# Attention scores on a half-filled systolic array: 32-row bands, with keys and queries kept a second time in turned bands

## The chip, the core and the metric

The kernel runs on one core of a Trainium2 chip. Its engines are TensorE (PE; its weight loads are listed apart as PEld), VectorE (DVE), ScalarE (ACT), GpSimd (POOL) and SyncE (SP, which only issues transfers). The metric is the device time of one launch in microseconds, lower is better.

## What is computed

One block of a network: cross-attention from 2048 queries to 1601 context rows with 8 heads of 4 numbers each, added to x behind a gate, and then a layer of 8 experts that each take their 512 best rows.

```python
q = _split_heads(queries @ Wq + bq)     # 8 heads, 4 numbers each
k = _split_heads(keys @ Wk + bk)
v = _split_heads(values @ Wv + bv)
scores = jnp.einsum('bhqd,bhkd->bhqk', q, k) * scale
attn = jax.nn.softmax(scores, axis=-1)
o = jnp.einsum('bhqk,bhkd->bhqd', attn, v)
...
x = x + jnp.tanh(g_xattn[0]) * attention(_layernorm(x), ctx_1024, ctx_1024, ...)
x = x + jnp.tanh(g_ffn[0]) * experts(_layernorm(x), ...)
```

## The kernel before

The heads are taken in two groups g of four. A head's query and key are each split into three bf16 parts, so that bf16 products give float32 scores; with the row of its maximum a head takes 32 of the 128 partitions, so a group fills the 128. The tile `qrows` holds the queries in that form and `kpad` the keys.

Work is cut into 16 units: four chunks c of 512 queries, in each two groups, in each two halves h of 256 queries. The four units of a chunk are numbered r = 0 to 3. A unit runs over 13 key tiles kt of 128 keys (the last has 65), and in each of them PE does this, in the order written in the main loop at the end of the block of PE:

- the maxima that are due (`max_tile`), in front of the scores and behind them. A unit has 16 of them (`TILES`), dealt out over the 13 key tiles by `tiles_by`, about one unit ahead of their use. Each is two matmuls of 401 keys that fill two PSUM banks; DVE reduces both at once into `mquart` and frees them. Two such pairs of banks are in use (`next_dve`).
- the scores (`scores`, twice: p = 0 and p = 1). Each call makes two heads' scores, 256 queries each, into one bank, from which ACT makes `probs` by one exp of 512 columns. ACT's work has three banks in rotation (`next_act`): the call waits until ACT has emptied the bank it used three takings ago.
- the weighted sum of the values (`pv`) for the key tile two back, four heads side by side.

A contraction over 64 rows uses half of PE's rows: `band(p)` is rows 0 to 63 or 64 to 127. Two heads lie in a band, so `kpad` holds the keys twice, each time with one of the two heads cleared; DVE clears for group 0 (in `keys_split`), ACT for group 1 (`pad_k1`).

When a unit's maxima are complete, DVE turns them into rows (`max_parts`), PE adds them to the queries (`place_max`, at kt = 10 of the unit before) and ACT stores the sum as `qfull` (`q_full`).

Beside this, at fixed places (r, kt), runs the work of the neighbour chunks: transposes and projection of the next queries (`XN_AT`, `Q_AT`), output projection (`WO_AT`), second normalisation, transposes of x2 and the router (`X2_AT`, `ROUTER_AT`). All engines are in-order queues with waits on semaphores; nothing is reordered by a scheduler. Transfers are issued by SP in the order written.

Of the kernel before, what the change touches and what calls it, by code (L numbers as in the profile page):

```python
# [17 lines left out]
P = 128  # L18
# [90 lines left out]
def build(nc, x, ctxt, g_x, g_f, Wq, bq, Wk, bk, Wv, bv, Wo, bo, rw, rb, w1, b1, w2, b2, cf, cdigits, out, x2d):  # L109
# [9 lines left out]
    with es:  # L119
# [33 lines left out]
        kpad = ar("kpad", [P, NG, 2, KEYS], BF16)  # L153
# [3 lines left out]
        qfull = ar("qfull", [P, NG, CW], BF16)  # L157
# [6 lines left out]
        krows = ar("krows", [P, 2, CW], BF16)  # L164
# [33 lines left out]
        with nc.sbuf_tensor("ctx_sb", [P, NKT, D], F32) as ctx_sb, nc.sbuf_tensor("ctxT", [P, KD, KEYS], F32) as ctxT:  # L198
# [70 lines left out]
        s_xf, s_c1, s_t1, s_c2, s_rows, s_kpad0, s_kpad1 = [sem(n) for n in (  # L269
            "qk_biased", "qk_high", "qk_rest", "qk_middle", "qk_rows", "k_padded_group0", "k_padded_group1")]  # L270
# [69 lines left out]
        def band(p):  # L340

            return slice(64 * p, 64 * p + 64)
# [53 lines left out]
        def _(sp):  # L396
# [22 lines left out]
            sp.dma_start(b2b[:, :, :], b2.rearrange("e h -> (e h)").partition_broadcast(P)).then_inc(s_b2, 16)  # L419
# [8 lines left out]

            for half in range(2):
                load_w1(0, half)  # L430
                load_w2(0, half)
            with sp.Fori(0, LAST) as c:
                sp.wait_ge(s_x1, c + 1)
                sp.dma_start(out_v[:, bass.ts(c, CT), :], xs[:, bass.ts(c, CT), :]).then_inc(s_out1, 16)
                sp.wait_ge(s_x2, c + 1)
                sp.dma_start(x2_v[:, bass.ts(c, CT), :], x2[:, :, :]).then_inc(s_x2st, 16)
# [23 lines left out]
        def _(pool):  # L460
# [46 lines left out]
            for b, (lo, w) in enumerate(KB):  # L507
                split_rest(pool, nc.gpsimd, 5 + b, (5 + b) % 2, w)
                pool.wait_ge(s_kpad0, 4)
                at_least(pool, s_kpad1, b - 1)  # L510
                split_rows(pool, nc.gpsimd, 5 + b, w, krows[:, b % 2, 0:w])
# [127 lines left out]
        def _(act):  # L639
# [66 lines left out]
            def pad_k1(j):  # L706

                lo, w = KB[j]
                act.wait_ge(s_rows, 5 + j + 1)
                for b in range(2):  # L710
                    last = nc.scalar.activation(kpad[:, 1, b, lo:lo + w], krows[:, j % 2, 0:w], ACT.Copy,
                                                scale=cst[:, C_HEAD + b:C_HEAD + b + 1])
                last.then_inc(s_kpad1, 1)

# [15 lines left out]
            pad_k1(3)  # L730
# [150 lines left out]
        def _(dve):  # L881
# [12 lines left out]
            for w, r in ((wk_sb, wkr), (wq_sb, wqr)):  # L894
                for k in range(KD):
                    for g in range(NG):
                        last = nc.vector.tensor_copy(
                            r[:, k, g, :].rearrange("p (h j d) -> p h j d", h=HG, d=HD)[:, :, 0:6, :],
                            w[:, k, 16 * g:16 * g + 16].rearrange("p (h d) -> p h d", d=HD).unsqueeze(2).to_broadcast([P, HG, 6, HD]))

            for g in range(NG):
                for k in range(KD):
                    nc.vector.tensor_copy(wkr[:, k, g, :].rearrange("p (h r) -> p h r", h=HG)[:, :, ROW_V:],
                                          wv_sb[:, k, 16 * g:16 * g + 16].rearrange("p (h d) -> p h d", d=HD))
                nc.vector.tensor_copy(bqkr[:, NG + g, :].rearrange("p (h r) -> p h r", h=HG)[:, :, ROW_V:],
                                      bias_sb[:, 64 + 16 * g:64 + 16 * g + 16].rearrange("p (h d) -> p h d", d=HD))
            for j in range(2):
                for g in range(NG):
                    last = nc.vector.tensor_copy(
                        bqkr[:, NG * j + g, :].rearrange("p (h j d) -> p h j d", h=HG, d=HD)[:, :, 0:6, :],  # L910
                        bias_sb[:, 32 * j + 16 * g:32 * j + 16 * g + 16].rearrange("p (h d) -> p h d", d=HD).unsqueeze(2).to_broadcast([1, HG, 6, HD]))
# [67 lines left out]
            def keys_split(j):  # L979

                lo, w = KB[j]
                split(j, j % 2, w, 2, krows[:, j % 2, 0:w])
                dve.wait_ge(s_rows, j + 1)
                for b in range(2):
                    last = nc.vector.tensor_scalar(kpad[:, 0, b, lo:lo + w], krows[:, j % 2, 0:w],
                                                   cst[:, C_HEAD + b:C_HEAD + b + 1], None, ALU.mult)
                last.then_inc(s_kpad0, 1)
# [22 lines left out]
            def max_tile(n):  # L1010

                u, j = divmod(n, TILES)
                t, a, kq = j // (2 * QUARTERS), j // QUARTERS % 2, j % QUARTERS
                dve.wait_ge(s_mm, n + 1)
                b = next_bank()
                nc.vector.tensor_reduce(mquart[:, u % 2, t, a, :, kq], ps[:, b:b + 2, 0:MAXW], AX.X, ALU.max).then_inc(s_mr, 1)  # L1016
                if j == TILES - 1:
                    max_parts(u)

            def max_parts(u):  # L1020

                dve.wait_ge(s_mr, TILES * (u + 1))
                at_least(dve, s_mpl, u)

                def spread(t, row):
                    return t[:, :, :, row].rearrange("p t (b a) -> p t a b", a=2)

                nc.vector.tensor_reduce(spread(mparts, KROW_M), mquart[:, u % 2, :, :, :, :], AX.X, ALU.max, negate=True)
                nc.vector.tensor_reduce(nmax[:, :, :].rearrange("p t (b a) -> p t a b", a=2), mquart[:, u % 2, :, :, :, :], AX.X, ALU.max,
                                        negate=True).then_inc(s_nm, 1)  # L1030
                dve.wait_ge(s_nm, u + 1)
                nc.vector.tensor_tensor(mparts[:, :, :, KROW_M + 1], nmax[:, :, :], mparts[:, :, :, KROW_M], ALU.subtract).then_inc(s_mp, 1)
# [306 lines left out]
        def _(pe):  # L1339
# [99 lines left out]
            def max_tile(n):  # L1439

                u, j = divmod(n, TILES)
                c, g, h, r = unit(u)
                t, a, kq = j // (2 * QUARTERS), j // QUARTERS % 2, j % QUARTERS
                if j == 0 and h == 0:
                    pe.wait_ge(s_rows, rows_of(c, g))
                if n < 4:
                    pe.wait_ge(s_kpad0, n + 1)
                    pe.wait_ge(s_xf, 4)
                if (c, g, h, j) == (0, 1, 0, 0):
                    pe.wait_ge(s_kpad1, 4)  # L1450
                bank = next_dve((s_mr, n + 1))
                lo, q = MAXSTEP * kq, CW * c + UW * h + P * t
                for b in range(2):
                    last = mm(ps[:, bank + b, 0:MAXW], qrows[band(b), g, q:q + P], kpad[band(b), g, a, lo:lo + MAXW], start=True, stop=True)  # L1454
                last.then_inc(s_mm, 1)

            def place_max(u):
# [5 lines left out]
                mm(ps[:, bank, 0:UW], ident_bf[:, :], qrows[:, g, q:q + UW], start=True, stop=False, skip_group_check=True)  # L1463
                for t in range(UQ):
                    last = mm(ps[:, bank, P * t:P * t + P], mparts[:, t, :, :].rearrange("p h r -> p (h r)"), ident_bf[:, :],
                              start=False, stop=True, skip_group_check=True)
                last.then_inc(s_mpl, 1)

            def scores(u, kt, p):
# [7 lines left out]
                last.then_inc(s_sc, 1)  # L1477

            def pv(u, kt):
# [7 lines left out]
                for hh in range(HG):  # L1487
                    last = mm(ps[32 * hh:32 * hh + 32, PV, 0:UW], vp[0:w, kt, g, hh, :], probs[0:w, step % PROBS, hh, :],  # L1488
                              start=(kt == 0), stop=(kt == NKT - 1))
# [92 lines left out]
            for u in range(UNITS):  # L1582
# [197 lines left out]
```

## Time and profile before

| | |
|---|---|
| median of 3 runs | 595.6 us (595.19 to 595.64) |
| the profiled execution | 594.75 us, of which its span is 592.9 us |
| PE busy | 551.4 us (93%) |
| DVE busy | 444.1 us (75%) |
| ACT busy | 397.4 us (67%) |
| POOL busy | 196.8 us (33%) |

The span has three parts: up to about 48 us loads, projections of keys and the first maxima; from 48 to 344 us the 16 attention units; then the choice of rows and the experts. The busy shares are means over parts with different limits, so the stretches have to be looked at one by one.

### The profile page before, as it was taken

Reading aid. Unit: us, or ns where it says so; the run is one execution under the profiler, and the core shown is the slowest. Engines: PE = TensorE matmul, PEld = TensorE weight load, DVE = VectorE, ACT = ScalarE, POOL = GpSimd, SP = SyncE. Lnnn points to the kernel's source line nnn. Section 1 sums busy time; section 2 is a strip of 40 time slices with the busy share of each in tenths; the row PEclk is TensorE's granted clock in tenths of the full one; section 3 lists DMA queues with packets and bytes.
Section 4 is the critical chain, followed back from the end, with each engine's and each line's share of the span. In section 5 each row is a group of like instructions: output and inputs, shape, how many; then the busy total and the mean of one; then the engine's idle time right before and its main releaser. Section 6 shows DMA issues by size and latency. Waiting matters only on the chain.

```text
span 592.9 us, 12821 instructions
## 1 busy us (share of the span) xinstructions
PE 551.4 (93%) x5043; PEld 318.6 (54%) x5043; DVE 444.1 (75%) x811; ACT 397.4 (67%) x774; POOL 196.8 (33%) x193
## 2 busy tenths in 40 slices
PE   6798899998999989999999998899999999999994
PEld 4433333333333333333333344469889898898974
DVE  3889879996798967989897258746767868677541
ACT  2587789987888878898888830044665646655651
POOL 3058030024420063400158010240735626346234
PEclk9999999999999999999999999999999999999998
DMA  8600000000000000000000004122735556356133
GB/s 280 241 2 1 1 1 3 2 1 38 2 36 2 2 37 1 37 2 1 37 38 2 36 19 140 34 60 72 163 112 117 144 136 148 108 107 163 16 36 35
DMA packets 23807, 35.80 MB, mean 60 GB/s; under 512 B 3459, under 2 KB 16196, under 8 KB 23620
## 3 DMA queue, kind: packets, MB, share of 16 engines
q1 hardware_dynamic: 17604, 26.59, 13.8%
q0 software_dynamic: 6144, 8.39, 8.3%
q8 instruction: 40, 0.66, 0.5%
q14 instruction: 19, 0.16, 0.1%
HBM read 26.59 MB, written 8.39 MB: 59 GB/s over the span
## 4 chain that ended last, share of the span: by engine, by line
PE 67%; DVE 18%; ACT 5%; issue 4%; POOL 3%; DMA 1%; POOLq 0%; ACTq 0%; DVEq 0%; SPq 0%
PE ps L1719 15%; PE ps L1726 15%; PE ps L1488 12%; DVE mquart L1016 11%; PE ps L1475 6%; PE ps L1454 6%; PE ps L1384 2%; ACT probs L741 2%; PE ps L1345 2%; POOL xn L528 2%; PE ps L1360 1%; PE ps L1697 1%; PE ps L1672 1%; ACT osb L641 1%; PE ps L1513 1%
## 5 line engine op out<-in xcount | busy, mean ns | idle before, releaser
L1016 DVE TENSOR_REDUCE mquart<-ps 128x2 f32<-128x802 f32 x256 | 241.9, 988 | 33.4 <-PE ps L1454 30.2
L741 ACT ACTIVATE probs<-ps 128x512 f32<-128x512 f32 (+1 forms) x416 | 222.9, 599 | 24.0 <-PE ps L1475 20.8
L1488 PE MATMUL ps<-probs,vp 128*32 128x256 f32 (+1 forms) x1664 | 132.7, 391 | 4.5 <-ACT osb L641 4.5
L1454 PE MATMUL ps<-kpad,qrows 64*128 64x401 bf16 x512 | 90.6, 337 | 3.7 <-DVE mquart L1016 3.1
L1475 PE MATMUL ps<-qfull,kpad 64*128 64x256 bf16 (+1 forms) x832 | 89.8, 272 | 2.8 <-ACT x L762 0.9
L1313 DVE TENSOR_TENSOR h1l<-hf,h1h 128x512 fp32r<-128x512 f32 x64 | 44.4, 693 | 56.0 <-ACT hf L868 56.0
L867 ACT ACTIVATE h1h<-ps,b1T 128x512 fp32r<-128x512 f32 x64 | 44.0, 687 | 53.8 <-PE ps L1719 53.6
L1726 PE MATMUL ps<-w2h,h1h 128*128 128x256 f32 x256 | 73.8, 288 | 2.2 <-DVE h1l L1313 1.5
L1726 PE MATMUL ps<-w2l,h1h 128*128 128x256 f32 x256 | 72.4, 283 | 0.0
L1726 PE MATMUL ps<-w2h,h1l 128*128 128x256 f32 x256 | 72.3, 283 | 0.0
L1475 PEld LDWEIGHTS ps<-qfull,kpad 64*128 64x128 bf16 (+1 forms) x832 | 38.9, 96 | 48.2 <-ACT probs L741 25.1
L611 POOL DMA_INDIRECT out<-eo,idx_put x32 | 56.3, 1759 | 25.1 <-ACT eo L877 15.9
L1454 PEld LDWEIGHTS ps<-kpad,qrows 64*128 64x128 bf16 x512 | 26.3, 93 | 66.0 <-DVE mquart L1016 31.8
L1488 PEld LDWEIGHTS ps<-probs,vp 128*32 128x32 f32 (+1 forms) x1664 | 33.3, 108 | 51.3 <-ACT probs L741 34.0
L1726 PEld LDWEIGHTS ps<-w2h,h1h 128*128 128x128 f32 x256 | 48.8, 191 | 6.6 <-issue 4.7
L1719 PE MATMUL ps<-tokh,w1h 128*128 128x512 f32 x128 | 51.0, 398 | 0.0
L1719 PE MATMUL ps<-tokh,w1l 128*128 128x512 f32 x128 | 50.4, 394 | 0.0
L1719 PE MATMUL ps<-tokl,w1h 128*128 128x512 f32 x128 | 49.9, 390 | 0.0
L1726 PEld LDWEIGHTS ps<-w2l,h1h 128*128 128x128 f32 x256 | 48.9, 191 | 1.3
L1726 PEld LDWEIGHTS ps<-w2h,h1l 128*128 128x128 f32 x256 | 48.9, 191 | 0.0
L589 POOL DMA_INDIRECT toks<-x_rows,idx_get x32 | 32.0, 999 | 36.0 <-DVE idx_get L1291 24.9
L868 ACT ACTIVATE hf<-ps,b1T 128x512 f32<-128x512 f32 x64 | 43.7, 683 | 0.0
(198 smaller groups left out, 682.3 us busy)
## 6 DMA issues: line engine op xcount, KB each, us to landing
w1raw<-in_L_ffn_w SPq DMA_DIRECT2D x16, 512.0 KB, 4.6
w2raw<-in_L_ffn_w SPq DMA_DIRECT2D x16, 512.0 KB, 4.7
xs<-in_x SPq DMA_DIRECT2D x4, 512.0 KB, 7.7
ctx_sb<-in_ctx SPq DMA_DIRECT2D x3, 512.0 KB, 5.8
out<-xs SPq DMA_DIRECT2D x3, 512.0 KB, 2.6
x_rows<-x SPq DMA_DIRECT2D x3, 512.0 KB, 2.6
b2b<-in_L_ffn_b SPq DMA_DIRECT2D x1, 1024.0 KB, 11.1
out<-xs SPq DMA_DIRECT2D x2, 256.0 KB, 2.0
```

What stands on the lines that cost most here:

```text
L589: nc.gpsimd.indirect_dma_start(out=toks[:, t, :], out_offset=None, in_=x2d, in_offset=bass.IndirectOffsetOnAxis(ap=idx_get[:, t:t + 1], ax ...
L611: nc.gpsimd.indirect_dma_start(out=out_rows, out_offset=bass.IndirectOffsetOnAxis(ap=idx_put[:, t:t + 1], axis=0), in_=eo[:, t, :], in_off ...
L741: nc.scalar.activation(out_p, ps[0:w, next_bank(), :], ACT.Exp, scale=float(SCALE)).then_inc(s_ex, 1)
L867: nc.scalar.activation(h1h[:, f, :], ps[:, bank, :], ACT.Relu, bias=bias).then_inc(s_hh, 1)
L868: nc.scalar.activation(hf[:, f % 2, :], ps[:, bank, :], ACT.Relu, bias=bias).then_inc(s_hf, 1)
L1016: nc.vector.tensor_reduce(mquart[:, u % 2, t, a, :, kq], ps[:, b:b + 2, 0:MAXW], AX.X, ALU.max).then_inc(s_mr, 1)
L1313: nc.vector.tensor_tensor(h1l[:, f, :], hf[:, f % 2, :], h1h[:, f, :].bitcast(F32), ALU.subtract).then_inc(s_hl, 1)
L1454: last = mm(ps[:, bank + b, 0:MAXW], qrows[band(b), g, q:q + P], kpad[band(b), g, a, lo:lo + MAXW], start=True, stop=True)
L1475: last = mm(ps[0:w, bank, UW * b:UW * b + UW], kpad[band(p), g, b, P * kt:P * kt + w], qfull[band(p), g, UW * h:UW * h + UW], start=True, ...
L1488: last = mm(ps[32 * hh:32 * hh + 32, PV, 0:UW], vp[0:w, kt, g, hh, :], probs[0:w, step % PROBS, hh, :], start=(kt == 0), stop=(kt == NKT - 1))
L1719: last = mm(ps[:, UP_BANKS[f % 3], :], w[:, k, P * f:P * f + P], r[:, k, :], start=(m == 0), stop=(m == len(terms) - 1))
L1726: last = mm(ps[:, bank, a:a + D], h[:, f, P * t:P * t + P], w[:, f, :], start=(f == 0 and m == 0 and a == 0), stop=(f == NF - 1 and m == 2 ...
```

## The change

Now a band has 32 rows, one head. The scores use the bands at rows 0 and 32 (`score_band`), the maxima the bands at rows 64 and 96 (`max_band`). As each head must appear in both halves, the keys are kept as made (`kbands`) and with the halves exchanged (`kturned`), the queries likewise (`qrows`, and `qturned` in its upper half); SP's transfers from SBUF to SBUF make the turned copies. The cleared copies `kpad` and the operations that make them are gone. `qfull` holds two pairs of heads side by side in 64 partitions, so `place_max` and `q_full` handle 512 columns of 64 rows instead of 256 of 128. A unit's maxima are taken for the unturned heads first.

```diff
+        def score_band(p):
+            return slice(32 * p, 32 * p + 32)
+        def max_band(b):
+            return slice(64 + 32 * b, 64 + 32 * b + 32)
...
+            def turn_keys(j, g):
+                lo, w = KB[j]
+                sp.wait_ge(s_rows, BLOCKS.index(("k", j, g)) + 1)
+                sp.dma_start(kturned[64:P, g, lo:lo + w], kbands[0:64, g, lo:lo + w]).then_inc(s_kup[g], 16)
+                sp.dma_start(kturned[0:64, g, lo:lo + w], kbands[64:P, g, lo:lo + w]).then_inc(s_kdown[g], 16)
+            def turn_queries(c, g):
+                sp.wait_ge(s_rows, rows_of(c, g))
+                if c > 1:
+                    sp.wait_ge(s_mm, TILES * (PER_CHUNK * (c - 2) + PARTS * (g + 1)))
+                sp.dma_start(qturned[64:P, g, c % 2, :], qrows[0:64, g, CW * c:CW * c + CW]).then_inc(s_qt[NG * (c % 2) + g], 16)
...
-            def pad_k1(j):
-                lo, w = KB[j]
-                act.wait_ge(s_rows, 5 + j + 1)
-                for b in range(2):
-                    last = nc.scalar.activation(kpad[:, 1, b, lo:lo + w], krows[:, j % 2, 0:w], ACT.Copy,
-                                                scale=cst[:, C_HEAD + b:C_HEAD + b + 1])
...
-                take(qfull[:, g, UW * h:UW * h + UW], ps[:, next_bank(), 0:UW], s_qf)
+                take(qfull[0:64, g, :, UW * h:UW * h + UW], ps[0:64, next_bank(), :].rearrange("p (v q) -> p v q", v=2), s_qf)
...
-                split(j, j % 2, w, 2, krows[:, j % 2, 0:w])
-                dve.wait_ge(s_rows, j + 1)
-                for b in range(2):
-                    last = nc.vector.tensor_scalar(kpad[:, 0, b, lo:lo + w], krows[:, j % 2, 0:w],
-                                                   cst[:, C_HEAD + b:C_HEAD + b + 1], None, ALU.mult)
+                split(j, j % 2, w, 2, kbands[:, 0, lo:lo + w])
...
-                    last = mm(ps[:, bank + b, 0:MAXW], qrows[band(b), g, q:q + P], kpad[band(b), g, a, lo:lo + MAXW], start=True, stop=True)
+                    rows = max_band(b)
+                    queries = qrows[rows, g, CW * c + q:CW * c + q + P] if a else qturned[rows, g, c % 2, q:q + P]
+                    keys = (kbands if a else kturned)[rows, g, lo:lo + MAXW]
+                    last = mm(ps[:, bank + b, 0:MAXW], queries, keys, start=True, stop=True)
...
-                bank = next_act((s_ex, 2 * (NKT * u + kt) + p + 1))
-                for b in range(2):
-                    last = mm(ps[0:w, bank, UW * b:UW * b + UW], kpad[band(p), g, b, P * kt:P * kt + w],
-                              qfull[band(p), g, UW * h:UW * h + UW], start=True, stop=True)
+                rows = score_band(p)
+                return mm(ps[0:w, bank, UW * v:UW * v + UW], (kturned if v else kbands)[rows, g, P * kt:P * kt + w],
+                          qfull[rows, g, v, UW * h:UW * h + UW], start=True, stop=True)
...
-                    scores(u, kt, 0)
-                    scores(u, kt, 1)
+                    first, second = score_bank(u, kt, 0), score_bank(u, kt, 1)
+                    scores(u, kt, 0, 0, first)
+                    scores(u, kt, 1, 0, second)
+                    scores(u, kt, 0, 1, first).then_inc(s_sc, 1)
+                    scores(u, kt, 1, 1, second).then_inc(s_sc, 1)
```

PE before, one key tile of unit 0 that has a maximum in front of the scores (`mquart`'s source, L1454) and one behind; the four L1475 are the scores, L1488 is `pv`, and `probs_ready` is the semaphore by which ACT gives banks and probabilities free.

```order
L1454 MATMUL ps<-kpad,qrows 128x401 [waits max_reduced]
L1454 MATMUL ps<-kpad,qrows 128x401
L1475 MATMUL ps<-qfull,kpad 128x256 [waits probs_ready]
L1475 MATMUL ps<-qfull,kpad 128x256
L1475 MATMUL ps<-qfull,kpad 128x256 [waits probs_ready]
L1475 MATMUL ps<-qfull,kpad 128x256
L1454 MATMUL ps<-kpad,qrows 128x401 [waits max_reduced]
L1454 MATMUL ps<-kpad,qrows 128x401
L1488 MATMUL ps<-probs,vp 32x256 [waits probs_ready]
L1488 MATMUL ps<-probs,vp 32x256 x3
```

The same key tile after the change (L1472 maxima, L1496 scores, L1512 `pv`):

```order
L1472 MATMUL ps<-kbands,qrows 128x401 [waits max_reduced]
L1472 MATMUL ps<-kbands,qrows 128x401
L1496 MATMUL ps<-qfull,kbands 128x256 [waits probs_ready]
L1496 MATMUL ps<-qfull,kbands 128x256
L1496 MATMUL ps<-qfull,kturned 128x256 x2
L1472 MATMUL ps<-kbands,qrows 128x401 [waits max_reduced]
L1472 MATMUL ps<-kbands,qrows 128x401
L1512 MATMUL ps<-probs,vp 32x256 [waits probs_ready]
L1512 MATMUL ps<-probs,vp 32x256 x3
```

The maxima stand where they stood. The wait that stood ahead of the third score matmul now stands ahead of the first, together with the first one's own.

SP after the change, from the end of the preparation to the first chunks' outputs (L441 to L449 are the turning transfers, L455 to L435 loads for the experts, L463 and L468 the stores of a chunk's x and x2):

```order
L449 DMA qturned<-qrows 64x512 [waits qk_rows]
L455 DMA b2b<-in_L_ffn_b 128x2048
L431 DMA w1raw<-in_L_ffn_w 128x2x512
L435 DMA w2raw<-in_L_ffn_w 128x4x256
L431 DMA w1raw<-in_L_ffn_w 128x2x512
L435 DMA w2raw<-in_L_ffn_w 128x4x256
L449 DMA qturned<-qrows 64x512 [waits qk_rows] x2
L463 DMA out<-xs 128x1024 [waits x1_ready]
L449 DMA qturned<-qrows 64x512 [waits max_scores,qk_rows] x2
L468 DMA x_rows<-x 128x1024 [waits ln2_out]
```

Before, the loads of `b2b`, `w1raw` and `w2raw` waited for nothing; now they stand behind 18 turning transfers, the last of which waits for the queries of group 1, and each chunk's store of x2 stands behind the turning of the queries two chunks on.

## Rows read from the trace of the kernel before

A row of a timeline has start and length in us, engine, line, operation, tiles, shapes, count and the idle time before it with what ended it. A row of windows has the stretch in us, its length, busy us (and instructions) of PE, PEld, DVE, ACT and POOL, granted clock, DMA share and GB/s. A row of the chain has start, length and what held it.

**Rows 1.** The page: busy times, and the chain that ended last.

```profile
PE 551.4 (93%) x5043; PEld 318.6 (54%) x5043; DVE 444.1 (75%) x811; ACT 397.4 (67%) x774; POOL 196.8 (33%) x193
PE 67%; DVE 18%; ACT 5%; issue 4%; POOL 3%; DMA 1%; POOLq 0%; ACTq 0%; DVEq 0%; SPq 0%
```

**Rows 2.** Windows of units 3, 4, 5, 10, 13 and 15, first exp to first exp.

```profile
105.26:120.72 15.46, 15.15 (x193) 5.54 (x193) 15.13 (x20) 14.54 (x28) 0.00 (x0) 1.00 0.01 2
120.72:142.98 22.26, 18.99 (x215) 7.83 (x213) 17.30 (x30) 16.91 (x33) 10.85 (x8) 1.00 0.01 1
142.98:163.85 20.87, 20.04 (x201) 7.15 (x199) 17.30 (x28) 17.79 (x35) 7.81 (x8) 1.00 0.07 27
240.66:258.81 18.15, 17.76 (x221) 7.41 (x220) 16.11 (x22) 15.83 (x32) 2.95 (x4) 1.00 0.08 31
292.85:309.56 16.71, 15.53 (x193) 5.42 (x191) 16.64 (x28) 14.59 (x29) 7.22 (x9) 1.00 0.09 34
327.37:343.10 15.73, 15.22 (x170) 5.65 (x168) 3.02 (x10) 14.25 (x29) 1.22 (x3) 1.00 0.10 35
```

**Rows 3.** Timeline of one key tile in unit 3: start, length, engine, work.

```profile
108.56 0.34 PE L1454 MATMUL ps<-kpad,qrows 64*128 64x401 bf16 x2
108.74 0.38 PE L1475 MATMUL ps<-qfull,kpad 64*128 64x256 bf16 x4
109.05 0.64 PE L1488 MATMUL ps<-probs,vp 128*32 128x256 f32 x8
109.15 2.15 ACT L741 ACTIVATE probs<-ps 128x512 f32<-128x512 f32 x4 [0.33 <-PE ps L1475]
109.62 0.34 PE L1454 MATMUL ps<-kpad,qrows 64*128 64x401 bf16 x2
```

**Rows 4.** Timeline of DVE around the end of unit 3's maxima.

```profile
116.44 0.20 DVE L1028 TENSOR_REDUCE mparts<-mquart 128x8 bf16<-128x32 f32 x1
...
116.84 4.67 DVE L1016 TENSOR_REDUCE mquart<-ps 128x2 f32<-128x802 f32 x5
```

**Rows 5.** The page's groups of DVE's reduces and ACT's exps: count, busy us, mean ns.

```profile
L1016 DVE TENSOR_REDUCE mquart<-ps 128x2 f32<-128x802 f32 x256 | 241.9, 988 | 33.4 <-PE ps L1454 30.2
L741 ACT ACTIVATE probs<-ps 128x512 f32<-128x512 f32 (+1 forms) x416 | 222.9, 599 | 24.0 <-PE ps L1475 20.8
```

**Rows 6.** Timeline of unit 15, where PE waits for ACT's banks.

```profile
341.18 1.55 ACT L741 ACTIVATE probs<-ps 128x512 f32<-128x512 f32 x3
...
341.82 0.14 PEld L1475 LDWEIGHTS ps<-qfull,kpad 64*65 64x65 bf16 x2 [0.21 <-ACT probs L741]
```

**Rows 7.** Timeline in unit 12: reduces in a row, then the placing of the maxima.

```profile
286.98 1.89 DVE L1016 TENSOR_REDUCE mquart<-ps 128x2 f32<-128x802 f32 x2
...
287.79 0.28 PE L1463 MATMUL ps<-qrows,ident_bf 128*128 128x256 bf16 x1
287.91 0.28 PE L1465 MATMUL ps<-ident_bf,mparts 128*128 128x128 bf16 x2
288.22 0.38 ACT L641 ACTIVATE qfull<-ps 128x256 bf16<-128x256 f32 x1
```

**Rows 8.** The chain that ended last, in the preparation.

```profile
17.76 0.54 DVE kpad L985 x2
...
21.95 0.35 DVE kpad L985
```

**Rows 9.** Timeline of unit 8 (as unit 4): the next chunk's queries.

```profile
212.35 0.63 PE L1378 MATMUL ps<-cst,xn 128*128 128x128 f32 x4 [1.44 <-POOL xn L528]
```

**Rows 10.** Timeline of unit 5 behind a projection of queries.

```profile
150.62 0.77 PE L1475 MATMUL ps<-qfull,kpad 64*128 64x256 bf16 x3 [0.22 <-ACT xf L654]
```

**Rows 11.** Timeline of unit 10, a key tile with a transpose of x2.

```profile
250.95 0.39 PE L1475 MATMUL ps<-qfull,kpad 64*128 64x256 bf16 x4
...
252.01 0.66 PE L1520 MATMUL ps<-cst,x 128*128 128x128 f32 x4
252.60 0.40 PE L1475 MATMUL ps<-qfull,kpad 64*128 64x256 bf16 x4
```

More of the change, by code:

```diff
@@ L338, in dve_bank, with place_of @@
             return 3 + 2 * (n % 2)
-        def band(p):
-            return slice(64 * p, 64 * p + 64)
+        def score_band(p):
+            return slice(32 * p, 32 * p + 32)
+        def max_band(b):
+            return slice(64 + 32 * b, 64 + 32 * b + 32)
+        def place_of(head):
+            return 2 * (head % 2) + head // 2
         PLACE = 10
@@ L893, in _ @@
             dve.wait_ge(s_wts, 96)
[L894 to L911, printed above, removed]
+            def heads(a, x):
+                return a.rearrange("p n (y x d) -> p n y x d", x=2, d=HD)[:, :, :, x, :]
@@ new lines, in places @@
+            def places(a, x):
+                return a.rearrange("p n (x y j d) -> p n x y j d", x=2, y=2, d=HD)[:, :, x, :, :, :]
+            w_in, w_out = [t[:, :, :].rearrange("p k (g c) -> p (k g) c", g=NG) for t in (wk_sb, wq_sb, wv_sb)], [
+                t[:, :, :, :].rearrange("p k g r -> p (k g) r") for t in (wkr, wqr)]
+            b_in = bias_sb[:, :].rearrange("p (n c) -> p n c", c=16)
+            for x in range(2):
+                for src, dst in zip(w_in, w_out):
+                    nc.vector.tensor_copy(places(dst, x)[:, :, :, 0:6, :], heads(src, x).unsqueeze(3).to_broadcast([P, KD * NG, 2, 6, HD]))
+                nc.vector.tensor_copy(places(w_out[0], x)[:, :, :, 7, :], heads(w_in[2], x))
+                nc.vector.tensor_copy(places(bqkr[:, NG:2 * NG, :], x)[:, :, :, 7, :], heads(b_in[:, 2 * NG:3 * NG, :], x))
+                last = nc.vector.tensor_copy(places(bqkr[:, :, :], x)[:, :, :, 0:6, :],
+                                             heads(b_in, x)[:, 0:2 * NG].unsqueeze(3).to_broadcast([1, 2 * NG, 2, 6, HD]))
@@ L1462, in place_max, with scores, score_bank @@
                 bank = next_act((s_qf, u + 1))
[L1463 to L1466, printed above, removed]
+                for v in range(2):
+                    mm(ps[0:64, bank, UW * v:UW * v + UW], ident_bf[:, 64 * v:64 * v + 64], qrows[:, g, q:q + UW],
+                       start=(v == 0), stop=False, skip_group_check=True)
+                    for t in range(UQ):
+                        last = mm(ps[0:64, bank, UW * v + P * t:UW * v + P * t + P], mparts[:, t, 2 * v:2 * v + 2, :].rearrange("p h r -> p (h r)"),
+                                  ident_bf[:, :], start=False, stop=True, skip_group_check=True)
                 last.then_inc(s_mpl, 1)
-            def scores(u, kt, p):
+            def scores(u, kt, p, v, bank):
                 c, g, h, r = unit(u)
                 w = kt_rows(kt)
-                bank = next_act((s_ex, 2 * (NKT * u + kt) + p + 1))
-                for b in range(2):
-                    last = mm(ps[0:w, bank, UW * b:UW * b + UW], kpad[band(p), g, b, P * kt:P * kt + w],
-                              qfull[band(p), g, UW * h:UW * h + UW], start=True, stop=True)
-                last.then_inc(s_sc, 1)
+                if (c, h, kt, p, v) == (0, 0, 0, 0, 1):
+                    pe.wait_ge(s_kdown[g], 64)
+                rows = score_band(p)
+                return mm(ps[0:w, bank, UW * v:UW * v + UW], (kturned if v else kbands)[rows, g, P * kt:P * kt + w],
+                          qfull[rows, g, v, UW * h:UW * h + UW], start=True, stop=True)
+            def score_bank(u, kt, p):
+                return next_act((s_ex, 2 * (NKT * u + kt) + p + 1))
             def pv(u, kt):
```

57 lines of the change are left out of this document (31 added, 26 removed).

## The prediction

> **What bounds the kernel now.** I read the page first. PE is busy 93% of the span and holds 67% of the chain that ended last, DVE 18% [rows 1]. That invites the thought that all of PE's saving comes back as time. So I cut the attention part into its 16 units and read the busy times of each [rows 2]. Four kinds appear.
>
> Units 2, 3, 7 and 11 carry little beside attention. Unit 3 takes 15.46 us with PE busy 15.15 and DVE 15.13. One key tile there, from maximum to maximum, takes 109.62 - 108.56 = 1.06 us: 0.18 us for the maximum pair, 0.31 us from the scores' start to `pv`, 0.57 us for `pv` [rows 3]. PE has no pause in it. DVE's floor is close by: two reduces in a row take 1.89 us and one takes 0.99 us, so their pitch is 0.90 us [rows 5, 7], and 16 of them with the 0.40 us that the end of a unit's maxima puts between two reduces [rows 4] make 14.8 us, or 1.14 us per key tile. PE is the bound by only 15.46 - 14.8 = 0.66 us.
>
> Units 6, 10 and 14 add transposes of x2 and the router. Unit 10 takes 18.15 us, with PE busy 17.76, DVE 16.11 [rows 2]. PE has some 2 us to give before DVE stops it.
>
> Units 4 and 8 wait for POOL: at 212.35 PE had stood 1.44 us until `xn` was there [rows 9]. Units 1, 5 and 9 hold two projections and the work of ACT behind them: at 150.62 the scores wait for ACT's `xf` [rows 10]. Units 0, 12 and 13 have DVE nearly full (unit 13: 16.64 of 16.71 us) [rows 2].
>
> Unit 15 has no maxima left to take; PE is busy 15.22 of 15.73 us [rows 2].
>
> **The change, part by part.** *Overlap.* A maximum pair now runs in row bands that the scores don't use. The pair took 0.18 us of PE's queue before the scores could start [rows 3]; if bands are independent, that goes to nothing for a maximum in front of the scores. Two matmuls in two bands do run side by side: the pair of maxima lasts 0.34 us together, and the group mean of one is the same size, since the next work starts 0.18 us after the first [rows 3]. Four side by side in row bands appear nowhere; below nothing (four bands slower than two in turn) I exclude, as the reads and banks are the same ones. The bounds are 0 and 0.18 us per maximum. I take 0.17 us in front of the scores and 0.06 us behind them, where the scores' second half covers only part.
>
> The Trainium skill (TensorE: Matmul & The Clock Gate, part 3) gives 3.07 times for four row tiles of 512 columns. By it four bands would return about three quarters of what I assume, and the sum would be some 0.5 us smaller, by an estimate from that page.
>
> *Order of the scores.* The alternation of bands brings nothing: the four score matmuls last 0.38 us [rows 3], one matmul of 401 columns 0.34 us. Had the second head of a band waited for the first, and the other band behind both, 256 more columns would show, about 0.18 x 256/401 = 0.11 us, so 0.49 us. The same page says that matmuls start and end strictly in program order, which with two heads per band gives three slots instead of two; by it the new order would save 0.11 us in each of 208 key tiles. The trace speaks against it.
>
> *The moved wait.* This is what costs. Before, the first two score matmuls of a key tile waited for a bank that ACT freed one and a half key tiles back; only the third waited for p = 0 of the key tile just before. Now the first waits for both. That closes a ring: exp of p = 0 (0.60 us [rows 5]), ACT's release to PE's weight load (341.18 + 0.60 = 341.78 to 341.82, 0.04 us [rows 6]), first score matmul to the next exp (109.15 - 108.74 = 0.41 us [rows 3]). Sum 1.05 us; with roundings I take 1.06. So a key tile with one maximum, which took 1.06 us by PE, takes 1.06 us by the ring. Only the three key tiles of a unit with two maxima gain (16 maxima over 13 key tiles), about 0.18 us each, until DVE stops them. Queued behind the waiting scores are a second maximum, `pv` and the next first maximum; DVE waits for those.
>
> Per unit, then. Ordinary (4 units): 3 x 0.18 = 0.54 us at most, and DVE leaves 0.66 us; DVE can't always use it with two pairs of banks, so I take half, 0.25 us: **-1.0 us**. Units 6, 10, 14: in the key tiles with transposes PE is the bound by much. The one shown goes from scores to scores in 252.60 - 250.95 = 1.65 us, 0.66 of it transposes [rows 11], so the ring doesn't bind and 0.17 to 0.23 us come back. Four such in a unit give 0.75 us; for three units I take **-2.0 us**, unit 14 less. Units 1, 4, 5, 8, 9: POOL, projections and ACT's work stay; **0**. Units 0, 12, 13: **0**. Unit 15: exps could follow each other there at a pitch of (1.55 - 0.60)/2 = 0.48 us [rows 5, 6], 0.95 us per key tile; by the ring 1.06 us. About five of its key tiles run near 0.97: 5 x 0.10 = **+0.5 us**.
>
> *Placing the maxima.* Six matmuls for three, 1024 columns for 512: 0.12 us (287.91 - 287.79) for 256 [rows 7], so 0.24 us more on PE, and `q_full` 512 columns for 256: 0.60 for 0.38 us. In the loop it stands beside exps, where its key tile is set by ACT's banks; in front of unit 0 nothing hides it: **+0.4 us**.
>
> *Preparation.* DVE's clearing of `kpad` lies on the chain: 0.54 us for the first block of keys [rows 8], and again for the next; from the second on only parts count, since ACT's projection of the queries ends almost at the same moment. The chain shifts by 0.54 to 0.9 us; I take **-0.7 us**. ACT's clearing of group 1 is beside PE's maxima: 0. DVE's fewer copies of weights lie under PE's warm-up matmuls: 0.
>
> *Turning.* Turned keys of group 0 are needed at the ninth maximum, turned queries 8 maxima (over 7 us) after the queries exist: hidden, unless a transfer takes over 7 us. The loads moved behind are for the experts, 290 us later. The stores of x2 stand behind the turned queries, but POOL makes those queries before that x2. All 0.
>
> Sum: -1.0 - 2.0 + 0.5 + 0.4 - 0.7 = **-2.8 us**. The profiled execution took 594.75 us, 0.85 below the median of the runs; so 592.0 for such an execution and **592.8 us** for the median.
>
> **The rivals.** (1) *PE's saving comes through more fully*: the ring hides behind spare time and units 1, 5, 9 gain as well. Ordinary units at DVE's 14.8 us give -2.6, units 6, 10, 14 -5, three of the projection units -0.5 each, preparation -0.3: about -9 us, 586.5. For it: PE's 67% of the chain. Against it: the ring is arithmetic of rows.
>
> (2) *The ring is longer than I think*, the slower side. It decides from 1.14 us per key tile, where it passes DVE's pace. It is only 0.08 us from there; a later start of the scores behind a maximum in flight would do. At 1.17 us an ordinary unit takes 13 x 1.17 = 15.2 us plus about 0.8 us for `osb` and `q_full`, 16.0: +0.5 us in nine units, +1 us in unit 15: +5.5 us less 0.3, 601.
>
> (3) *Gains and losses cancel*: DVE takes what PE gives in ordinary units, and ACT's catching up behind projections (0.95 us per key tile) is slowed to 1.06 in units 1, 5, 9: 595 to 596.
>
> (4) *The bands don't overlap in fours*: no gain in the loop, the place's 0.24 us of PE in each of 16 units: +3 us, 598.5.
>
> (5) *The new order saves a slot*: 208 x 0.11 us less on PE, held by DVE: near 586.
>
> **How the numbers follow.** Changes under 0.2% (1.2 us) can't be told from none here. Forecast (590 to 594.4) 0.42; rivals 1 and 5 (below 590) 0.12 and 0.02; rival 3 0.19; rival 2 0.18; rival 4 0.07. Faster 0.56, same 0.19, slower 0.25. The range leaves out the outer parts of rivals 1 and 2: 588 to 599; the forecast's own is 590 to 594.4.
>
> **What would show it.** In units 2, 3, 7, 11 key tiles with one maximum at 1.05 to 1.08 us, PE idle before the scores and released by exps; PE's busy share of unit 3 down from 15.15 to about 13 us. Scores starting within 0.02 us of a maximum in front. Unit 10 near 17.4 us, unit 15 near 16.2 us, first exp at about 47.9 us for 48.2. I am wrong if scores still start 0.18 us behind a maximum, if the ring lasts over 1.14 us, or if units 1, 5 and 9 move by over 0.5 us.

## The result, and the profile after

The changed kernel takes 602.5 us (four runs, 602.15 to 606.14) against 595.4 us before: 1.013 times as long, 95% interval 1.010 to 1.017. The forecast was 592.8 us in a range of 588 to 599. The profiled execution is the longest of the four, 606.14 us at a mean granted clock of 0.975; the others stood at 0.987. Ratios and intervals below leave out runs that took over 1.5% longer than the fastest of their kernel.

The page of the kernel after, the same two rows as [rows 1]:

```profile
PE 545.7 (90%) x5091; PEld 314.4 (52%) x5091; DVE 441.9 (73%) x795; ACT 399.7 (66%) x766; POOL 197.2 (33%) x193
PE 71%; DVE 10%; ACT 8%; issue 6%; POOL 3%; DMA 1%; POOLq 0%; ACTq 0%; DVEq 0%; SPq 0%
```

PE is busy 5.7 us less and the span is 11.4 us longer. DVE's share of the chain fell from 18% to 10%: the engine that was to be the next bound was not reached. ACT's rose from 5% to 8% and "issue" from 4% to 6%, which would fit a loop of waits between PE and ACT.

Windows of the kernel after, the same columns and the same units as [rows 2] (3, 4, 5, 10, 13, 15), and unit 8 between them:

```profile
107.47:123.14 15.67, 14.64 (x198) 5.29 (x202) 15.21 (x20) 14.76 (x28) 0.00 (x0) 1.00 0.01 2
123.14:145.51 22.37, 18.06 (x220) 7.37 (x220) 17.29 (x30) 17.21 (x33) 10.86 (x8) 1.00 0.00 1
145.52:166.80 21.28, 17.91 (x208) 6.24 (x210) 17.17 (x28) 18.26 (x35) 8.13 (x8) 1.00 0.10 33
200.96:227.09 26.13, 22.11 (x216) 8.56 (x216) 17.11 (x30) 17.50 (x34) 10.85 (x8) 0.78 0.04 18
248.99:267.49 18.50, 17.59 (x227) 7.19 (x231) 16.17 (x22) 16.21 (x33) 2.88 (x4) 1.00 0.08 31
302.37:319.77 17.40, 15.69 (x196) 5.45 (x194) 17.11 (x28) 14.77 (x29) 6.92 (x8) 0.95 0.08 32
338.26:354.93 16.67, 14.38 (x169) 5.42 (x169) 3.02 (x10) 14.83 (x29) 0.97 (x2) 1.00 0.09 34
```

Two things are to be seen. Where the granted clock is 1.00, each of these units is a little longer than before: unit 3 by 0.21 us, 4 by 0.11, 5 by 0.41, 10 by 0.35, 15 by 0.94. And the clock is no longer 1.00 everywhere. Units 4 and 8 do the same work; at 0.78 unit 8 takes 3.8 us more. Before, all these windows stood at 1.00.

The timeline of unit 3 after, four key tiles (compare [rows 3]; PEld's row is the weight load of the first two score matmuls, with the time that PE's weight loads stood idle before it, in brackets, and what ended it):

```profile
113.03 0.29 PE L1496 MATMUL ps<-qfull,kbands 32*128 32x256 bf16 x2
113.05 0.34 PE L1472 MATMUL ps<-kturned,qturned 32*128 32x401 bf16 x2
113.14 0.29 PE L1496 MATMUL ps<-qfull,kturned 32*128 32x256 bf16 x2
113.36 0.64 PE L1512 MATMUL ps<-probs,vp 128*32 128x256 f32 x8
114.15 0.12 PEld L1496 LDWEIGHTS ps<-qfull,kbands 32*128 32x128 bf16 x2 [0.64 <-ACT probs L760]
114.18 0.28 PE L1496 MATMUL ps<-qfull,kbands 32*128 32x256 bf16 x2 [0.19 <-ACT probs L760]
...
115.34 0.28 PE L1496 MATMUL ps<-qfull,kbands 32*128 32x256 bf16 x2
...
116.49 0.28 PE L1496 MATMUL ps<-qfull,kbands 32*128 32x256 bf16 x2
```

The scores start at 113.03, 114.18, 115.34 and 116.49: 1.15 us apart whatever stands between them, where [rows 3] showed 1.06. At 114.15 it is ACT that PE has waited for. The overlap itself works: two score matmuls, two maxima behind them and the other two score matmuls start within 0.11 us, from 113.03 to 113.14, and the maxima last 0.34 us as they did alone.

### The profile page after: what moved, and what is told of

Read it like the earlier page. It is cut to its first block, busy times and chain, and to the rows that moved or that the text cites. A ratio compares the mean times of both kernels' runs of the same rounds, so it can differ in the third digit from the quotient of the medians.

```text
span 604.3 us, 13106 instructions
## 1 busy us (share of the span) xinstructions
PE 545.7 (90%) x5091; PEld 314.4 (52%) x5091; DVE 441.9 (73%) x795; ACT 399.7 (66%) x766; POOL 197.2 (33%) x193
## 4 chain that ended last, share of the span: by engine, by line
PE 71%; DVE 10%; ACT 8%; issue 6%; POOL 3%; DMA 1%; POOLq 0%; ACTq 0%; DVEq 0%; SPq 0%
PE ps L1746 15%; PE ps L1753 15%; PE ps L1512 12%; PE ps L1496 7%; PE ps L1472 6%; DVE mquart L1030 5%; ACT probs L760 5%; PE ps L1398 3%; PE ps L1359 2%; PE ps L1374 2%; POOL xn L558 2%; PE ps L1724 1%; PE ps L1699 1%; PE ps L1482 1%; PE ps L1537 1%
## 5 line engine op out<-in xcount | busy, mean ns | idle before, releaser
L760 ACT ACTIVATE probs<-ps 128x512 f32<-128x512 f32 (+1 forms) x416 | 225.8, 596 | 29.1 <-PE ps L1496 21.7
L1512 PE MATMUL ps<-probs,vp 128*32 128x256 f32 (+1 forms) x1664 | 137.0, 402 | 5.6 <-ACT osb L671 5.6
L1496 PE MATMUL ps<-qfull,kbands 32*128 32x256 bf16 (+1 forms) x416 | 60.5, 280 | 20.6 <-ACT probs L760 16.1
L1496 PE MATMUL ps<-qfull,kturned 32*128 32x256 bf16 (+1 forms) x416 | 60.6, 275 | 0.0
L1512 PEld LDWEIGHTS ps<-probs,vp 128*32 128x32 f32 (+1 forms) x1664 | 33.8, 109 | 51.1 <-issue 28.8
L1496 PEld LDWEIGHTS ps<-qfull,kbands 32*128 32x128 bf16 (+1 forms) x416 | 24.6, 93 | 67.9 <-ACT probs L760 36.8
L1472 PE MATMUL ps<-kturned,qturned 32*128 32x401 bf16 x256 | 43.4, 340 | 2.9 <-DVE mquart L1030 2.9
L1472 PE MATMUL ps<-kbands,qrows 32*128 32x401 bf16 x256 | 45.1, 357 | 0.9 <-DVE mquart L1030 0.7
```

Of the source, the lines that this page charges most:

```text
L760: nc.scalar.activation(out_p, ps[0:w, next_bank(), :], ACT.Exp, scale=float(SCALE)).then_inc(s_ex, 1)
L1472: last = mm(ps[:, bank + b, 0:MAXW], queries, keys, start=True, stop=True)
L1496: return mm(ps[0:w, bank, UW * v:UW * v + UW], (kturned if v else kbands)[rows, g, P * kt:P * kt + w], qfull[rows, g, v, UW * h:UW * h + U ...
```

## The experiments

Two theories stood first: the ring of waits that the prediction describes, only longer than it says; or 32-row bands that are slow in themselves. The clock came third. Units are compared from one profiled execution of each kernel.

**Split waits.** In the changed kernel, band 0's two score matmuls are issued before the second bank is waited for. This also puts the four score matmuls back into the order that they had before:

```diff
-                    first, second = score_bank(u, kt, 0), score_bank(u, kt, 1)
-                    scores(u, kt, 0, 0, first)
-                    scores(u, kt, 1, 0, second)
-                    scores(u, kt, 0, 1, first).then_inc(s_sc, 1)
-                    scores(u, kt, 1, 1, second).then_inc(s_sc, 1)
+                    for p in range(2):
+                        bank = score_bank(u, kt, p)
+                        scores(u, kt, p, 0, bank)
+                        scores(u, kt, p, 1, bank).then_inc(s_sc, 1)
```

> The changed kernel, with the two score matmuls of band 0 issued after their own bank is free, then the wait for the second bank, then the two of band 1. Ring theory (each key tile takes exp 0.60 us, 0.13 us to the scores, 0.41 us to the next exp = 1.15 us): the ring now spans one and a half key tiles, so units 3, 7 and 11 fall from 15.67 us to DVE's 14.8 to 15.2 us, unit 15 from 16.67 to about 15.3 us, and the whole to 587 to 593 us. Rival, 32-row bands are slow in themselves: key tiles stay near 1.15 us and the time near 602 us.

Measured: eight runs of 593.2 to 595.6 us at mean clocks of 0.982 to 0.988 (median 594.1), and two of 603.7 and 604.1 us at 0.963 and 0.966; the median of all ten is 594.6 us. The eight give 0.9975 of the kernel before (0.9963 to 0.9988). The ring theory holds, since the bands are as narrow as in the changed kernel, and the other falls. Timeline of PE in unit 3 of this kernel:

```profile
112.47 0.34 PE L1472 MATMUL ps<-kturned,qturned 32*128 32x401 bf16 x2
112.47 0.36 PE L1496 MATMUL ps<-qfull,kbands 32*128 32x256 bf16 x2
...
113.44 0.34 PE L1472 MATMUL ps<-kturned,qturned 32*128 32x401 bf16 x2
...
114.16 0.34 PE L1472 MATMUL ps<-kturned,qturned 32*128 32x401 bf16 x2 [0.22 <-DVE mquart L1030]
...
115.00 0.29 PE L1496 MATMUL ps<-qfull,kbands 32*128 32x256 bf16 x2
115.06 0.34 PE L1472 MATMUL ps<-kbands,qrows 32*128 32x401 bf16 x2
115.13 0.28 PE L1496 MATMUL ps<-qfull,kturned 32*128 32x256 bf16 x2
```

A key tile with one maximum now takes 113.44 - 112.47 = 0.97 us, near ACT's 0.95. Maximum and scores start in the same hundredth. At 114.16 PE waits for DVE to free banks, the limit that the prediction named. Unit 3 takes 15.25 us (expected: at most 15.2) and unit 10 17.55 us. The whole stayed above the expected 587 to 593 us. The profiled run shows five stretches of 3.4 us at half clock in the attention part, one of them in unit 15. That unit missed its 15.3 us at full clock too: with the fillers below, at clock 1.00, it takes 15.9 us from its first exp to the end of its last, as before the change.

**One wait for two.** The changed kernel with the order kept, but one wait ahead of the scores where one semaphore frees both banks (the later value implies the earlier):

```diff
+                if n >= 3 and act_readers[n - 3][0] is not act_readers[n - 2][0]:
+                    pe.wait_ge(*act_readers[n - 3])
+                if n >= 2:
+                    pe.wait_ge(*act_readers[n - 2])
```

> The changed kernel, with one wait in front of a key tile's scores instead of two: where both banks are freed by the same semaphore, only the later value is waited for. If the second of two waits costs 0.06 to 0.09 us at each start (0.04 us from release to weight load before, 0.10 us after), key tiles fall from 1.15 to 1.06 to 1.09 us, unit 15 from 16.67 to about 16 us, the whole by 6 to 9 us to about 594. If the start is slow for another reason (narrow bands, a change of tile shape behind pv), nothing moves: 1.15 us, 602 us.

Measured: 600.6 us (1.0079, 1.0060 to 1.0098). Timeline of PE, unit 3:

```profile
112.38 0.28 PE L1496 MATMUL ps<-qfull,kbands 32*128 32x256 bf16 x2
...
113.46 0.28 PE L1496 MATMUL ps<-qfull,kbands 32*128 32x256 bf16 x2
...
114.53 0.28 PE L1496 MATMUL ps<-qfull,kbands 32*128 32x256 bf16 x2
```

1.08 and 1.07 us per key tile for 1.15. The second wait costs 0.07 us each time it is on the ring. Unit 3 takes 15.27 us for 15.67, unit 15 0.4 us less. The gain of the whole, 1.9 us, is smaller than the expected 6 to 9. The clock has part in it: all four runs stood at 0.979 to 0.981, where the changed kernel had 0.987 in most, and in the profiled run units 0, 4 and 5 hold stretches at half clock and take 0.9 to 1.7 us more than the same units do at full clock with two waits.

**The moved wait alone, in the kernel before.**

```diff
-                    scores(u, kt, 0)
-                    scores(u, kt, 1)
+                    first, second = [next_act((s_ex, 2 * (NKT * u + kt) + p + 1)) for p in range(2)]
+                    scores(u, kt, 0, first)
+                    scores(u, kt, 1, second)
```

> The kernel before, with nothing changed but that both banks of a key tile are waited for ahead of its first score matmul. Ring theory: key tiles go from 1.06 to 1.10 to 1.15 us as in the changed kernel and those with two maxima keep 1.24 us, so unit 3 goes from 15.46 to about 16.0 us and the whole to 602 to 606 us. Rival, bands: the wait is not what costs, under 1 us more than before.

Measured: 602.9 us (1.0121, 1.0104 to 1.0138). Timeline of PE, unit 3:

```profile
111.59 0.40 PE L1474 MATMUL ps<-qfull,kpad 64*128 64x256 bf16 x4
...
112.71 0.15 PEld L1474 LDWEIGHTS ps<-qfull,kpad 64*128 64x128 bf16 x4 [0.47 <-ACT probs L741]
112.74 0.40 PE L1474 MATMUL ps<-qfull,kpad 64*128 64x256 bf16 x4
...
113.89 0.29 PE L1474 MATMUL ps<-qfull,kpad 64*128 64x256 bf16 x2
```

The same 1.15 us, with bands of 64 rows. This one edit costs 7.5 us, as much as the whole change, and at a clock of 0.994 to 0.995 in all four runs. So the four kernels form a square: without the ring 595.4 us (wide bands) and 594.1 (narrow), with it 602.9 and 602.5. The narrow bands bring little in the whole either way, with what the clock takes from them included; in unit 3, with the ring in both and at clock 1.00, they bring 0.3 us (15.67 for 15.95).

**The same with one wait.** The previous edit, with the two banks taken as in "one wait for two".

> The kernel before with both banks taken ahead of the first score matmul, but by one wait where both banks are freed by the same semaphore. With two waits a key tile took 1.15 us here too. If the second wait costs 0.07 us whatever the bands are, key tiles come to 1.08 us and the time to about 597 us (602.9 with two waits, 595.4 before). If the 0.07 us belongs to narrow bands, it stays at 602 to 603 us.

Measured: 600.8 us (1.0088, 1.0073 to 1.0102). Key tiles come to 1.08 us, so the 0.07 us does not belong to narrow bands. But the whole stays 5.3 us over the kernel before and not 1.6: units 3, 7 and 11 are back at 15.5 us, while units 14 and 15 keep 0.7 us each, and units 5, 6, 9 and 10 0.4 to 0.5 us. These are units in which PE's scores used to follow each other faster behind inserted work: in unit 15 four key tiles stood at 0.89 to 0.90 us before and none is under 1.06 here. The first exp of the profiled run also comes 1.1 us later than before the change, which the ring does not explain.

**No overlap.** Split waits, but the maxima in the score bands:

```diff
-            return slice(64 + 32 * b, 64 + 32 * b + 32)
+            return slice(32 * b, 32 * b + 32)
...
-                sp.dma_start(qturned[64:P, g, c % 2, :], qrows[0:64, g, CW * c:CW * c + CW]).then_inc(s_qt[NG * (c % 2) + g], 16)
+                sp.dma_start(qturned[0:64, g, c % 2, :], qrows[64:P, g, CW * c:CW * c + CW]).then_inc(s_qt[NG * (c % 2) + g], 16)
...
```

> As the split waits, but the maxima run in the score bands (rows 0 and 32) and so can't lie beside the scores. If four bands side by side are worth 0.17 us for each maximum in front of the scores, this is slower than the split waits by 4 to 10 us and near the kernel before (595 to 600 us); if the overlap is worth nothing, both are alike within 1 us.

Measured: four runs of 598.7, 606.6, 608.3 and 619.7 us at mean clocks of 0.994, 0.976, 0.972 and 0.947; they are too far apart for an interval. Its units at full clock can be compared with those of the split waits: 16.26 for 15.65 us (unit 2), 15.52 for 15.25 (3), 21.09 for 20.41 (5), 18.37 for 17.55 (10), 15.74 for 15.23 (7). So the overlap is worth 0.3 to 0.8 us in a unit, and without it these units take 0.1 to 0.2 us more than in the kernel before. Windows of this kernel, then of the kernel before, in the same stretch:

```profile
214.50:238.40 23.90, 23.86 (x134) 8.78 (x134) 9.07 (x11) 11.85 (x22) 4.60 (x2) 0.50 0.06 24
```

```profile
214.50:238.40 23.90, 22.54 (x217) 8.65 (x218) 17.42 (x29) 19.82 (x39) 8.24 (x8) 1.00 0.06 23
```

For 24 us PE is granted half clock, 1.2 GHz, and its rows show it busy without a pause (their ends are modelled); PE, not DVE, is then the bound. Just before the clock falls PE stands 1.44 us, until `xn` is there; in the kernel before it stands as long in the same place and the clock stays at 1.00.

**Fillers.** Split waits, with full-array matmuls of no use where PE waits in units 4, 8 and 12:

```diff
+            def fill(bank, n):
+                for _ in range(n):
+                    mm(ps[:, bank, :].rearrange("p (r c) -> p r c", c=P), ident_bf[:, :], ident_bf[:, :].unsqueeze(1).to_broadcast([P, 4, P]), start=True, stop=True)
...
                         even = next_act((s_wt, 2 * (c - 1) + 1))
+                        fill(even, 2)
...
-                        transpose_xn(c + 1, k, next_act((s_Tt, KD * (c + 1) + k + 1)))
+                        bank = next_act((s_Tt, KD * (c + 1) + k + 1))
+                        if c > 0:
+                            fill(bank, (5, 1)[k])
+                        transpose_xn(c + 1, k, bank)
```

> The split waits, with full-array matmuls of no use put where PE waits in units 4, 8 and 12 (5 ahead of the first transpose of the next queries, 1 ahead of the second, 2 ahead of the output projection). If the stretches of half clock that the split-waits run shows near 135, 204, 217 and 303 us follow PE's pauses there, fewer of them are left, units 4 and 8 return from 23.4 to about 22.3 us and the time goes from 594.6 to 590 to 593 us. If the clock falls for another reason, nothing changes, or the fillers cost about 1 us.

Measured: 592.7 us, 0.9954 of the kernel before (0.9941 to 0.9968), the fastest of all; its six runs lie between 591.9 and 593.8 us at mean clocks of 0.989 to 0.993 (split waits without fillers: 0.982 to 0.988 and 594.1 us). One stretch at half clock is left in the attention part of the profiled run, for five. Unit 4 takes 22.57 us for 23.41. This is as expected if the clock follows PE's pauses there.

**All maxima in front.** Split waits, with a key tile's second maximum ahead of the scores too:

```diff
-                    for n in range(tiles_by(u, 2 * kt - 1), tiles_by(u, 2 * kt)):
+                    for n in range(tiles_by(u, 2 * kt - 1), tiles_by(u, 2 * kt + 1)):
                         max_tile(n)
```

> The split waits, with all maxima of a key tile in front of its scores. If the overlap is the limit, a second maximum in front is hidden as well (0.11 us in 3 key tiles of a unit, up to 5 us in all). If DVE's two pairs of banks are the limit, the scores now wait behind a maximum that has no bank, and the time is 2 to 10 us longer than the split waits.

Measured: 596.9 us (1.0023, 1.0010 to 1.0037; twelve runs), 2.8 us over the 594.1 of the split waits. An ordinary unit takes 15.54 us for 15.25. Timeline of PE, unit 3:

```profile
110.61 0.34 PE L1472 MATMUL ps<-kturned,qturned 32*128 32x401 bf16 x2
111.15 0.34 PE L1472 MATMUL ps<-kturned,qturned 32*128 32x401 bf16 x2 [0.19 <-DVE mquart L1030]
111.15 0.28 PE L1496 MATMUL ps<-qfull,kbands 32*128 32x256 bf16 x2
```

The second maximum waits for DVE to free its banks, and the scores stand behind it until 111.15: DVE's banks are the limit.

**Fillers in the changed kernel.** The same fillers, with the ring left in.

> The changed kernel with the same fillers. The ring stays at 1.15 us. If about 2 to 4 us of its loss in a typical run is clock in units 4, 8 and 12, it goes from 602.5 to 598.5 to 600.5 us; if the clock there doesn't matter, it stays at 602 to 603 us.

Measured: 602.3 us (1.0121, 1.0106 to 1.0135) at mean clocks of 0.986 to 0.994: nothing gained in the median. Units 4 and 8 take 22.66 us in the profiled run, where they took 22.37 (clock 1.00) and 26.13 us (0.78) without. The fillers cost 0.3 us in a unit that needs none. That this cancels what they give is argued and not measured.

**Narrow maxima in the kernel before.** The same maxima over the 32 rows that hold data, in the same place, in place of 64 rows half cleared:

```diff
-                    last = mm(ps[:, bank + b, 0:MAXW], qrows[band(b), g, q:q + P], kpad[band(b), g, a, lo:lo + MAXW], start=True, stop=True)
+                    rows = slice(64 * b + 32 * a, 64 * b + 32 * a + 32)
+                    last = mm(ps[:, bank + b, 0:MAXW], qrows[rows, g, q:q + P], kpad[rows, g, a, lo:lo + MAXW], start=True, stop=True)
```

> The kernel before, with one difference: each maximum matmul contracts over the 32 rows of its head instead of 64 rows of which 32 are cleared, in the same place and order. Nothing waits longer. If matmuls over fewer rows are what lets the clock fall, stretches of half clock appear in the attention part, the mean clock is under 0.99 in some runs and the time 1 to 10 us over 595.4. If the clock follows PE's pauses alone, or the scores' rows or the placing matter, nothing changes: clock 0.995 to 0.997, 595.4 us within 1 us.

Measured: 606.9, 606.9, 612.9 and 619.8 us at mean clocks of 0.996, 0.996, 0.982 and 0.964; ratio 1.025 (1.019 to 1.031). Two effects lie in this. With the clock at 0.996 it is already 11.7 us slower, which neither theory expected. Timeline of PE:

```profile
114.26 0.40 PE L1476 MATMUL ps<-qfull,kpad 64*128 64x256 bf16 x4
114.59 0.34 PE L1455 MATMUL ps<-kpad,qrows 32*128 32x401 bf16 x2
114.86 0.64 PE L1489 MATMUL ps<-probs,vp 128*32 128x256 f32 x8
115.43 0.40 PE L1476 MATMUL ps<-qfull,kpad 64*128 64x256 bf16 x4
```

A key tile takes 115.43 - 114.26 = 1.17 us for 1.06. The maxima start 0.33 us behind the scores; in the kernel before, where they have 64 rows like the scores, they start 0.21 to 0.23 us behind them. So going from 64-row to 32-row tiles costs 0.1 us. And in two of four runs the mean clock is 0.982 and 0.964; in the kernel before it was never under 0.991.

**Fillers without overlap.** The no-overlap kernel with the fillers.

> The kernel with 32-row bands, split waits and maxima in the score bands, now with the fillers in units 4, 8 and 12. Its run without them at a mean clock of 0.994 took 598.7 us, at 0.976 606.6. If the fillers keep the clock, all runs lie at 598.5 to 600 us; if they don't, they spread from 599 to 620 us as before.

Measured: 604.2 to 604.4 us in three runs (clock 0.984) and 620.7 and 620.8 in two (0.945); ratio 1.0154 (1.0134 to 1.0175). The fillers do not keep the clock. In the profiled run (620.8 us) units 4, 8 and 12, which have fillers, stand at 1.00; the clock falls in units 0, 1 and 15, where there are none. Window from unit 0 into unit 1:

```profile
52.70:86.80 34.10, 33.91 (x220) 10.64 (x220) 20.18 (x24) 16.69 (x31) 7.00 (x5) 0.50 0.17 61
```

## Why the prediction was wrong

**The step that failed is the length of the ring**, in "the moved wait". The prediction had the ring, its parts and the point at which it decides (1.14 us, DVE's pace), and put it at 1.06 us. It is 1.15 us: taking it out gives back the time (split waits), putting it in alone costs 7.5 us (the moved wait in the kernel before). The exp's 0.60 us and the 0.41 us from the first score matmul to the next exp were right. What was too short is ACT's release to PE's start. Timeline of the changed kernel, with two waits in front of the first score matmul:

```profile
114.59 0.60 ACT L760 ACTIVATE probs<-ps 128x512 f32<-128x512 f32 x1
...
115.31 0.12 PEld L1496 LDWEIGHTS ps<-qfull,kbands 32*128 32x128 bf16 x2
115.34 0.28 PE L1496 MATMUL ps<-qfull,kbands 32*128 32x256 bf16 x2
```

And of "one wait for two":

```profile
112.80 0.60 ACT L760 ACTIVATE probs<-ps 128x512 f32<-128x512 f32 x1
...
113.45 0.10 PEld L1496 LDWEIGHTS ps<-qfull,kbands 32*128 32x128 bf16 x2
113.46 0.28 PE L1496 MATMUL ps<-qfull,kbands 32*128 32x256 bf16 x2
```

From the exp's end to the score matmul it is 0.15 us with two waits and 0.06 us with one. The prediction took 0.04 us, to the weight load, from a row with a single wait [rows 6], and so put the second wait at nothing. Of the 0.09 us by which the ring came out longer, 0.07 is the second wait (1.15 to 1.08 us, in bands of 32 and of 64 rows alike) and 0.02 was missing with one wait already.

Rival 2, given 0.18, had the mechanism, though not its reason (a maximum in flight). Its price of 601 us is near partly by luck: it stands for a ring of 1.17 us. Worked out in the same way for 1.15 us (13 x 1.15 + 0.8 = 15.75 us, so +0.3 us in nine units, +0.8 in unit 15, less 0.3) it would be about 599, an estimate. The rest is clock and a larger loss in units with inserted work than it counted.

**The term "ordinary units, -1.0 us"** became +0.8 us: units 2, 3, 7 and 11 grew by 0.16 to 0.25 us. In unit 3 eleven of 13 key tiles stand at 1.15 to 1.17 us, just over DVE's 1.14.

**Units 6, 10, 14, "-2.0 us"**: +1.4 us. The prediction counted on key tiles with transposes, in which PE is the bound. In unit 10 these gave back 0.3 us in all and not 0.75, and the others lost more: single ones went from 1.06 to 1.17 us and the last one of the unit from 1.35 to 1.63.

**Unit 15, "+0.5 us"**: +0.9 us, same cause. **Units 1, 5, 9, "0"**: +0.4 us in unit 5, at full clock. **Units 4 and 8, "0"**: +0.1 us in unit 4, at full clock. **Units 0, 12 and 13, "0"**: +1.0, +0.7 and +0.7 us, with one stretch at half clock in unit 0 and one across 12 and 13. The reason given there, DVE nearly full, was also misread for unit 12: DVE is busy 16.01 of its 18.53 us before.

**The clock was not in the prediction at all.** In the profiled run 24 us of the attention part are granted at half speed. Units 8 and 9 against their like, 4 and 5, give 3.8 and 0.6 us; units 0 and 1 took 1.0 and 1.1 us less in the filler kernel with the same ring. That is some 6.5 of the 12.4 us by which the 16 units grew. The other 5.9 are the ring and whatever the stretch in units 12 and 13 costs, which no run separates. The other runs of the changed kernel have a mean clock of 0.987 for 0.975 and take 3.3 to 4.0 us less, so in the median some 3 us of 7.1 would be clock (6.5 less 3.6). The fillers in the changed kernel speak for less: its profiled run, with one stretch left (mean clock 0.994), still took 602.0 us, 0.6 us of it for fillers in units 4 and 8. So 1 to 3 us is an estimate, not a measurement.

**What was right.** Four bands run side by side with no loss to be seen: the maxima's 0.18 us vanish. The Trainium skill (TensorE: Matmul & The Clock Gate, part 3) gives 3.07 times for four, at 512 columns, which no run here has; at 256 and 401 columns the matmuls kept their 0.28 and 0.34 us. DVE is the next bound: with split waits PE waits for it (0.22 us in the row at 114.16). With those the units come to 15.25 us (unit 3, forecast 15.2) and 17.55 us (unit 10, forecast 17.4). But this is partly luck: the forecast had single key tiles at 1.06 us by the ring, and without the ring they take 0.90 to 1.07. In the same way the fillers' kernel, 592.7 us, comes to the number that was forecast and not by the way that was forecast. That alternating bands would bring nothing fits the rows: in the split-waits kernel the order in the queue is `kbands`, `kturned`, `kbands`, `kturned`, and the timeline shows both `kbands` at 115.00 and both `kturned` at 115.13. PE starts a matmul of a free band ahead of an earlier one whose band is taken, so PE does not work strictly in the order of its queue, which corrects what stands ahead of the prediction for all engines. The Trainium skill (TensorE: Matmul & The Clock Gate, part 3) says that matmuls start strictly in program order, and the measurement decides against it. The preparation can't be judged: the first exp came between 47.6 and 49.2 us in kernels of the new layout, and between 48.2 and 49.3 in those of the old. Turning was hidden: no engine is shown waiting for a turning transfer, and these landed in about 2 us, in the median.

**What stays open.** Why the clock falls. Every profiled run with 32-row scores has a stretch at half clock in the attention part, the kernel before and its two variants with 64-row bands have none, and with narrow maxima alone two of four runs had a lower clock. PE's pauses alone don't sort these kernels. Windows of the attention part of the kernel before, of the moved wait alone, of the split waits and of no overlap:

```profile
48.19:343.22 295.03, 278.25 (x3199) 106.06 (x3195) 246.24 (x356) 252.89 (x493) 83.32 (x78) 1.00 0.04 14
48.76:351.92 303.16, 278.47 (x3199) 108.70 (x3196) 247.40 (x356) 256.14 (x493) 83.31 (x78) 1.00 0.04 14
48.63:344.23 295.60, 272.66 (x3242) 100.71 (x3238) 243.99 (x352) 251.11 (x493) 83.36 (x78) 0.97 0.07 26
48.96:355.50 306.54, 291.17 (x3244) 112.17 (x3240) 246.76 (x352) 255.83 (x493) 83.33 (x78) 0.96 0.07 25
```

PE is idle for 16.8 and 24.7 us in the first two, at clock 1.00, and for 22.9 and 15.4 us in the last two, at 0.97 and 0.96. Which property counts, and why a stretch lasts 3 us in one run and 34 us in another, these runs don't tell.

## What to carry to other kernels

When an edit takes two resources where it took one at a time, write down the loop that closes: who frees the second one, what that engine waits for, and the sum once around. If the sum is near the pace of the present bound (here 1.06 forecast and 1.15 measured, against 1.14), it is the risk of the change, however much work was removed. Take the price of each wait in it from a row with the same number of waits. And if matmuls get narrower, look at the granted clock of each stretch before comparing times.

## What was not expected of the hardware

- A second wait in front of the same matmul adds 0.07 us to PE's start, although its condition is met one exp before that of the other.
- Going between row tiles of 64 and 32 rows costs PE 0.1 us, in a kernel whose matmuls otherwise stayed the same: they start 0.33 us behind the scores for 0.22.
- PE was granted half clock for 23.9 and 34.1 us while its rows show it busy for 23.86 and 33.91 us. The Trainium skill (TensorE: Matmul & The Clock Gate, part 1) says that idling throttles the clock and sustained activity releases it; here it was not released for as long as that with PE shown busy.
